# Full attention: values weighed for eight query blocks at once, with inverses kept in DRAM

## The reference, cut to what matters

```python
qkv = x @ w_qkv.T
qkv = qkv.reshape(b, t, dh, 3, h).transpose(3, 0, 4, 1, 2)     # t = 1024, h = 16 heads, dh = 64
q, k, v = (qkv[0], qkv[1], qkv[2])
scores = jnp.einsum('bhid,bhjd->bhij', q, k) * scale
rel = jnp.arange(t)[None, :] - jnp.arange(t)[:, None] + (t - 1)
bias = rel_bias[rel]                      # 255 rows; larger indices take the last row
scores = scores + bias.transpose(2, 0, 1)[None]
attn = jax.nn.softmax(scores, axis=-1)
out = jnp.einsum('bhij,bhjd->bhid', attn, v)
out = out.transpose(0, 2, 1, 3).reshape(b, t, h * dh)
return out @ w_out.T                      # x = x + ga * this
```

## Time and profile before

| what | value |
|---|---|
| median of three runs | 2606.95 us |
| lowest and highest | 2600.77 and 2609.22 us |
| the profiled execution | 2595.65 us |
| its span | 2593.9 us |
| busy over the whole span | PE 94%, DVE 83%, ACT 78%, POOL 59% |
| mean granted TensorE clock | 0.986 |

### The profile page before, as it was taken

One profiled execution on the slowest core, in us unless ns is written; L12 is line 12 of the kernel. 1 busy time (PEld: TensorE's weight loads), 2 busy tenths in 40 slices (PEclk: granted clock), 3 DMA queues, 4 the chain that ended last, 5 costly groups with the idle time before them and its releaser, 6 DMA issues. The chain is left out here.

```text
span 2593.9 us, 118567 instructions
## 1 busy us (share of the span) xinstructions
PE 2449.6 (94%) x52349; PEld 1966.9 (76%) x52349; DVE 2153.8 (83%) x2455; ACT 2034.3 (78%) x4077; POOL 1519.8 (59%) x1029
## 2 busy tenths in 40 slices
PE   6799999999999999999999999699999999997999
PEld 2478888888888888888888887467776776775787
DVE  5888888888888888888888886489898888885898
ACT  4788898889889899988888996667676666664776
POOL 3788887888888888888888884122222222222110
PEclk9999999999999999999999999899999999999999
DMA  3244433443444344334443332123232322221221
GB/s 96 51 99 94 109 78 93 94 108 84 98 94 111 82 94 99 95 84 94 101 97 83 91 85 60 43 48 68 46 70 50 67 47 66 51 57 31 83 74 41
DMA packets 275793, 202.01 MB, mean 78 GB/s; under 512 B 117568, under 2 KB 215880, under 8 KB 274248
## 3 DMA queue, kind: packets, MB, share of 16 engines
q1 hardware_dynamic: 275280, 194.42, 31.3%
HBM read 36.96 MB, written 1.11 MB: 15 GB/s over the span
## 5 line engine op out<-in xcount | busy, mean ns | idle before, releaser
L514 POOL TENSOR_TENSOR lt_t_sin<-lt_qk,lt_tab 128x512 f32<-128x512 f32 x384 | 685.1, 1805 | 225.1 <-DVE lt_qk L1296 222.8
L519 POOL TENSOR_TENSOR lt_qr<-lt_qr,lt_t_sin 128x1024 f32<-128x1024 f32 x192 | 457.7, 2384 | 28.1 <-POOL lt_t_sin L514 0.9
L2078 DVE TENSOR_REDUCE fa_neg_max<-bank 128x1 f32<-128x1024 f32 x256 | 301.6, 1220 | 90.7 <-PE bank L1875 89.1
L2000 ACT ACTIVATE fa_prob<-bank,fa_neg_max 128x1024 f32<-128x1024 f32 x128 | 142.6, 1114 | 215.7 <-DVE fa_neg_max L2078 163.4
L1901 PE MATMUL bank<-fa_prob_t,fa_v 32*64 32x128 f32 x16384 | 293.4, 276 | 16.8 <-issue 12.2
L1901 PEld LDWEIGHTS bank<-fa_prob_t,fa_v 32*64 32x64 f32 x16384 | 244.4, 130 | 78.1 <-issue 57.9
L2088 DVE STREAM_TRANSPOSE fa_prob_t<-fa_prob 128x1024 f32<-128x1024 f32 x256 | 302.1, 1218 | 0.0
L607 PE MATMUL bank<-lt_w_high,lt_x_high 128*128 128x512 f32 x576 | 262.2, 455 | 0.8 <-ACT lt_v_tok L1009 0.4
L977 ACT COPY lt_qk<-bank 128x512 f32<-128x512 f32 x384 | 224.5, 589 | 23.8 <-POOL lt_t_sin L514 2.8
L1296 DVE TENSOR_TENSOR lt_qk<-lt_qk,lt_rn 128x2048 f32<-128x2048 f32 x96 | 238.2, 2481 | 2.5 <-ACT lt_rn L1003 2.5
L1289 DVE TENSOR_REDUCE lt_ssq<-lt_qr 128x32 f32<-128x2048 f32 x96 | 218.9, 2281 | 24.7 <-ACT lt_qr L985 24.7
(11 more groups left out here) (260 smaller groups left out, 5857.0 us busy)
## 6 DMA issues: line engine op xcount, KB each, us to landing
lt_v<-lt_v_tok SPq DMA_DIRECT2D x576, 128.0 KB
fa_v<-fa_v_tok SPq DMA_DIRECT2D x256, 128.0 KB
lt_v<-lt_v_tok SPq DMA_DIRECT2D x192, 64.0 KB
lt_k_t<-lt_k_t SPq DMA_DIRECT2D x84, 128.0 KB, 2.9
lt_v<-lt_v SPq DMA_DIRECT2D x168, 64.0 KB, 2.1
lt_w_raw<-in_lt_wqkv_dram SPq DMA_DIRECT2D x36, 256.0 KB
ex_cw_all<-cw_kept SPq DMA_DIRECT2D x8, 1024.0 KB, 4.6
lt_x_s<-h_in SPq DMA_DIRECT2D x96, 64.0 KB, 2.8
```

What stands on the lines that cost most here:

```text
L514: pool.tensor_tensor(dst[:, :, i, :], src[:, :, 1 - i, :], tab[:, g // 2 % 2, 1, at:at + 32].unsqueeze(1).to_broadcast([P, HEADS, 32]), AL ...
L519: pool.tensor_tensor(qr[:, g % 2, half], qr[:, g % 2, half], t_sin[:, :], ALU.add).then_inc(S.rotated, 1)
L2078: dve.tensor_reduce(neg_max[:, u % 2, par:par + 1], bank[:, 2 * par:2 * par + 2, :].rearrange("p a n -> p (a n)"), AX.X, ALU.max, negate=T ...
```

## The change

`weigh_v` now takes a whole half at a time, one half later: half h = u // 8 - 1 is weighed in step u, four blocks of 32 keys in each step, with 256 moving columns (eight units of 32 queries). Accumulation is cut into three parts that end with the steps t = 2, 5 and 7 (`LASTS`); after each ACT copies 128x1024 out of banks 4 to 7 (into `h_mid`, a tile that is free in this layer), and POOL adds the copies (`add_att`). Weighing is not cut in pieces any more, and side jobs always follow it.

`prob_t` holds one half, with turned probabilities laid out by unit in even halves and by group of keys in odd ones, so that the units of the next half can take the places that weighing has just freed; `turn(u)` waits for the weighing of step u. The inverses of a half are turned in one 128x32 transposition and go to DRAM and back, broadcast to 64 partitions for each head, issued by SP behind `place_v`; widening, spreading by PE and their emptying on ACT go away. Jobs and outputs are at other steps and banks, and the stage has 146 steps instead of 136. The core of the diff:

```diff
-    UPQ = 4
-    QUADS = UNITS // UPQ
-    QPH = QB // UPQ
+    LASTS = (2, 5, 7)
+    OUTS = N // 256
     KB = N // 32
+    KBS = KB // QB
...
-        prob_t = buf("prob_t", [P, 2, 2, UPQ, N])
-        att = buf("att", [P, 4, P])
-        att_t = buf("att_t", [P, 2, CH])
+        prob_t = buf("prob_t", [P, 2, QB, QB, P])
+        att_t = buf("att_t", [P, 2, N])
...
+            half, t = u // QB + 1, u % QB
+            if half >= HALVES or t in (1, 5):
                 return []
-            first = JPH * half + 6 * (q % QPH) + max(0, 2 * (s - 1))
+            first = JPH * half + 2 * (0, 0, 1, 2, 3, 0, 4, 5)[t]
             return [first, first + 1]
 
         def outs_at(u):
-            q = u // UPQ - 2
-            return [2 * q, 2 * q + 1] if u % UPQ == 1 and 0 <= q < QUADS else []
+            half = u // QB - (3 if u % QB == 1 else 2)
+            first = OUTS * half + (2 if u % QB == 1 else 0)
+            return [first, first + 1] if u % QB in (1, 5) and 0 <= half < HALVES else []
...
+        def att_done(u):
+
+            return 3 * (u // QB - 1) + LASTS.index(u % QB) + 1
+
+        def att(part):
+            return h_mid[:, part, PAD:PAD + N].rearrange("p (a n) -> p a n", a=4)
...
+            if weighed_at(u) is not None and u % QB in LASTS:
+                eng.wait_ge(S.att, att_done(u))
...
+        STEPS = range(UNITS + 2 * QB + 2)
...
+                def widen_inverse(half):
+                    sp.wait_ge(S.inv_t, half + 1)
+                    if half >= 1:
+                        sp.wait_ge(S.inv_in, 32 * half)
+                    for a in range(4):
+                        sp.dma_start(inv_kept[:, 32 * a:32 * a + 32], inv_t[32 * a:32 * a + 2 * QB, :]).then_inc(S.inv_kept, 16)
+                    sp.wait_ge(S.inv_kept, 64 * (half + 1))
+                    if half >= 1:
+                        sp.wait_ge(S.att_t, half)
+                    for par in range(2):
+                        kept = inv_kept[QB * par:QB * par + QB, :].rearrange("(o u) q -> o (u q)", o=1)
+                        sp.dma_start(inv_all[HD * par:HD * par + HD, :], kept.to_broadcast([HD, N])).then_inc(S.inv_in, 16)
...
+                def add_att(half, n):
+                    pool.wait_ge(S.att, 3 * half + n + 1)
+                    if n == 2:
+                        pool.wait_ge(S.att_sum, 2 * half + 1)
+                    pool.tensor_tensor(att(0), att(0), att(1), ALU.add).then_inc(S.att_sum, 1)
+
+                def divide(half):
+                    pool.wait_ge(S.att_sum, 2 * half + 2)
+                    pool.wait_ge(S.inv_in, 32 * (half + 1))
+                    if half >= 2:
+                        pool.wait_ge(S.out, OUTS * (half - 1))
+                    pool.tensor_tensor(att_t[:, half % 2, :].rearrange("p (u a r) -> p a u r", u=QB, a=4),
+                                       att(0).rearrange("p a (u r) -> p a u r", u=QB),
+                                       inv_all[:, :].rearrange("p (u a r) -> p a u r", u=QB, a=4),
                                        ALU.mult).then_inc(S.att_t, 1)
...
+                def weigh_v(half, t):
+
+                    if t == 0:
+                        pe.wait_ge(S.turned, 2 * QB * (half + 1))
+                        pe.wait_ge(S.v, 256 * (half + 1))
+                    for i in range(KBS):
+                        kb, cols = KBS * t + i, slice(32 * i, 32 * i + 32)
                         for a in range(4):
                             rows = slice(32 * a, 32 * a + 32)
                             for par in range(2):
                                 d = slice(HD * par, HD * par + HD)
-                                mm = pe.matmul(bank[d, 4 + a, 0:P].rearrange("p (u r) -> p u r", u=UPQ),
-                                               v[rows, half % 2, kb, d],
-                                               prob_t[rows, q % 2, par, :, 32 * kb:32 * kb + 32],
-                                               start=kb == 0, stop=kb == KB - 1, skip_group_check=True)
-                    if n == 1:
-                        mm.then_inc(S.av, 1)
-
-                def spread_inverse(q):
-                    pe.wait_ge(S.wide_t, q + 1)
-                    if q == 0:
-                        pe.wait_ge(S.mean, 1)
-                    for a in range(4):
-                        rows = slice(32 * a, 32 * a + 32)
-                        for par in range(2):
-                            d = slice(HD * par, HD * par + HD)
-                            mm = pe.matmul(bank[d, 4 + a, P:2 * P].rearrange("p (u r) -> p u r", u=UPQ), mean_32[rows, :],
-                                           inv_t[rows, par, :, :], start=False, stop=True, skip_group_check=True)
-                    mm.then_inc(S.inv_all, 1)
+                                p = prob_t[rows, par, t, :, cols] if half % 2 else prob_t[rows, par, :, t, cols]
+                                mm = pe.matmul(bank[d, 4 + a, 0:JW].rearrange("p (u r) -> p u r", u=QB),
+                                               v[rows, half % 2, kb, d], p, start=i == 0 and t - 1 in (-1,) + LASTS,
+                                               stop=i == KBS - 1 and t in LASTS, skip_group_check=True)
+                    mm.then_inc(S.av, 1)
...
+                    half = weighed_at(u)
+
+
+                    fresh = u % QB in LASTS or half is None
                     if u + 1 < UNITS:
                         scores(u + 1)
                     wait_emptied(pe, u - 1)
-                    if s == 0:
-                        for j in jobs_at(u):
-                            job(j, fresh)
...
+                def empty_att(half, part):
+                    if half >= 1 and part < 2:
+                        act.wait_ge(S.att_t, half)
+                    if part == 2:
+                        act.wait_ge(S.att_sum, 2 * half + 1)
+                    act.copy(att(min(part, 1)), bank[:, 4:8, 0:JW]).then_inc(S.att, 1)
...
+                    half, j = u // QB, u % QB
+                    if half >= 1:
+                        dve.wait_ge(S.av, QB * (half - 1) + j + 1)
                     for par in range(2):
                         dve.wait_ge(S.probs, 3 * u + 1 + 2 * par)
-                        dve.transpose(prob_t[:, q % 2, par, u % UPQ, :], prob[:, u % 2, par, :]).then_inc(S.turned, 1)
-
-                def invert(q):
-
-                    r = row_sum[:, q % 2, :, :]
-                    dve.wait_ge(S.probs, 3 * UPQ * (q + 1))
+                        if half % 2:
+                            dve.transpose(prob_t[:, par, :, j, :], prob[:, u % 2, par, :].rearrange("p (g n) -> p g n", g=QB))\
+                               .then_inc(S.turned, 1)
...
+                def turn_inverse(half):
+                    dve.wait_ge(S.inv, half + 1)
+                    if half == 0:
+                        dve.wait_ge(S.cleared, 1)
+                    else:
+                        dve.wait_ge(S.inv_kept, 64 * half)
+                    dve.transpose(inv_t[:, :], inv_sum[:, :]).then_inc(S.inv_t, 1)
```

More of the change, by code:

```diff
@@ L1818, in add @@
                     pool.tensor_tensor(x, x, y[:, n % 2, :], ALU.add).then_inc(S.x, 1)
-                pool.memset(mean_32[:, :], 1.0 / 32).then_inc(S.mean, 1)
                 for i in LOWS:
@@ L1823, in _ @@
                 for u in STEPS:
-                    if u % UPQ == 1:
-                        if weighed_at(u) is not None:
-                            widen(weighed_at(u))
-                        for n in outs_at(u):
-                            add(n)
-                    if u % UPQ == 3 and weighed_at(u) is not None:
-                        divide(weighed_at(u))
+                    for n in outs_at(u):
+                        add(n)
                     for j in jobs_at(u):
@@ L1886, in scores @@
                     mm.then_inc(S.scores, 1)
-                def weigh_v(q, s, n):
-                    half = q // QPH
-                    lo, step = KB // UPQ * s, KB // UPQ // 2
-                    if s == 0 and n == 0:
-                        pe.wait_ge(S.turned, 2 * UPQ * (q + 1))
-                        if q % QPH == 0:
-                            pe.wait_ge(S.v, 256 * (half + 1))
-                    for kb in range(lo + step * n, lo + step * (n + 1)):
+                def weigh_v(half, t):
[4 more added lines that the diff above has]
+                        kb, cols = KBS * t + i, slice(32 * i, 32 * i + 32)
                         for a in range(4):
@@ L1926, in project_out @@
+                    mm.then_inc(S.av, 1)
+                def project_out(n, start):
+                    half = n // OUTS
+                    pair = half // B
+                    pe.wait_ge(S.att_t, half + 1)
+                    if n % (OUTS * B) == 0:
+                        pe.wait_ge(s_wo[pair % 2], 16 * (pair // 2 + 1))
+                    pe.matmul(out_bank(n), w_out[:, pair % 2, :], att_t[:, half % 2, n % OUTS * JW:n % OUTS * JW + JW],
```

(22 more changed lines are left out.)

135 lines of the change are left out of this document (40 added, 95 removed).

## The result

| what | before | after |
|---|---|---|
| median of six runs, same chip | 2601.18 us | 2629.34 us |
| lowest and highest | 2599.34 and 2609.22 | 2622.06 and 2637.63 |
| ratio, 95% interval | | 1.0099 [1.008, 1.0118] |
| the profiled execution, its span | 2595.65, 2593.9 us | 2625.08, 2623.3 us |

A forecast was written before the change was run, and what follows sets the result against it. Plain steps were taken as bound by the loop maxima, exponentials, scores, maxima (4.94 us). Steps -5.0, pauses -6.8 and tail +12.5 gave +0.7, or 2607.7 on the median, stated as 2606 us, range 2590 to 2626.

The forecast's parts named there:

- k1: Period between DVE's maxima in each half, holding sums and reciprocals: 5.39 us predicted, 5.00 before.
- k2: The next period of a half, PE's because weighing was cut around other matmuls: from 5.12 to 4.94 us.
- steps otherwise: Undisturbed half of eight periods: 42.20 us against 42.53, -0.33 each, -5.0 over 15 halves.
- tail: Stage end, where nothing covers weighing: eight steps instead of four, 33.1 us against 21.3, with 0.7 of pauses +12.5.
- rival E: Weighing cost is per record, 0.92 us a step instead of 1.76; faster, chance together with rival B 0.33.
- k7: Last period of a half, PE's because weighing was cut around other matmuls: from 5.36 to 4.94 us.
- rival B: Pauses vanish as PE uses code at half the rate, and emptying waits hide: -13.8, 2593 us, chance 0.29.
- Rival C: Pauses are not the code's, so none goes: +7.5, 2614 us, chance 0.14.
- Head: Stage start, where weighing begins four steps later and PE's longer rest may keep the clock low: 0, between -1 and +1.
- D: Odd halves' transposes, written as eight pieces, take 2.1 instead of 1.2 us: about +90, 2697 us, chance 0.06.
- F: The transposes' new wait for weighing decides in all steps, plain ones 5.17 us: +32, 2638 us, chance 0.10.
- A: The terms hold as summed: 2606 us, no change, chance 0.37.

The follow-up runs named there:

- one input: The changed kernel with DVE's two-input addition of row sums made a one-input reduction at the same place: 2595.60 us, ratio to before 0.9973.
- 128 columns: The changed kernel with each 256-column weighing matmul written as two of 128 columns: 2656.43 us, ratio to before 1.0199.
- head work: The changed kernel with inverses made in step 4, not 0, of a half, plus four unused PE matmuls in each of steps 1 to 7: 2586.00 us, ratio 0.9943.

## Why the prediction was wrong

**The step that failed** is that of k1: "so DVE has 2.49+2.27+0.46 and a transposition ... 5.39", together with "POOL ... Not on the path, except at the end". The 0.46 for sums and reciprocals was read in before, where POOL had nothing of length to do at that moment. The change puts a division of 2.36 us there, started by the last part sum, and DVE's addition of two SBUF operands stands until it ends: 1.75 instead of 0.13. k1 measured 7.05. With the hold taken away and nothing else, k1 is 5.43 (one input), and the sum of a half 42.00 against the 42.20 predicted. That this is the cause is shown by three repairs that touch different sides of it, and by the same hold planted in the kernel before. The Trainium skill has the rule (SBUF — State Buffer, SBUF: two separate sides): VectorE and GpSimd share a pair of ports that is locked for the whole instruction, taken by a VectorE operation with two SBUF inputs too, when the GpSimd operation reads SBUF, as the division does. The trace agrees to 0.03 us. It spoke against this change and was not weighed; the prediction asked of POOL only whether it was busy too much, not when.

**The account.** In us of the stage, relative to before; the sums of clean halves are those of one input:

| term | predicted | measured | worked out from |
|---|---|---|---|
| hold of the addition | 0 | +22.7 | 14 x (7.05 - 5.43) |
| slow scores in k2 | 0 | +8.6 | 7 halves, 42.8 instead of 7 x 4.88 |
| steps otherwise | -5.0 | -7.4 | 14 x (42.00 - 42.53) |
| disturbances, pauses for issue above all | -6.8 | -14.9 | 610.36 - 14 x 42.53 |
| first two halves | 0 | +3.0 | 49.22 - 47.06, 42.86 - 42.00 |
| tail | +12.5 | +16.4 | 44.9 - 28.5 |
| sum | +0.7 | +28.4 | stage: +28.6 |

**Slow scores** were in no step and no rival: PE's rest of 2.15, itself made by the hold, is followed in half of the cases by scores at the lower clock (granted 0.50). Without the rest they are gone from all halves (one input).

**Steps otherwise:** right within 0.2 of a half. Weighing of 64 records takes 1.98 in the profile where the old run of 128 took 2.10, as taken (the stream, not the record: rival E fell). The waits for the copies are 0.5 and cost what was said in k1 (with one input 5.43 for 5.39). Splits and spreading gave their time back (k2 4.88, k7 5.00).

**Pauses:** the direction was right, the size was not. "If pauses go with the code, 0.45 of 15.0" took them as in proportion; all went. The 15.0 is also more than the pauses: PE's waits for issue between unit 8 and unit 120 are 11.4 in 14, and the other 3.6 are longer periods for which no single cause was traced. That all went is rival B's first half. Rival C falls: the pauses went with half of the weighing's instructions and came back with them at 128 columns. That it is the fetching of the code that PE waits for fits, but is not shown. Nor are pauses in proportion to the code: 1.31 MB had none at all and 2.23 MB had 13.2 us. The Trainium skill's rule is that crossing a block of code is mostly hidden (Runtime: NRT & Kernel Launch, Instruction fetch mechanics). The changed kernel's trace agrees in full. Those of before and of 128 columns agree for most blocks, with 14 waits of PE for 132 pieces of all engines' code between unit 8 and unit 120 in the one, and 11 for 127 in the other, and these few are worth 11 to 14 us.

**Inverses through DRAM** cost nothing, as predicted; the broadcast lands in 4.0 us and no engine waits for it, not even when it starts four steps later.

**Head:** "I take 0, between -1 and +1" was +2.2, outside. The direction of the risk was named (a longer rest may keep the lower clock), and head work shows that the clock matters there. The size is that of one execution: the same work took 48.3 to 52.1 in the others.

**Tail:** 37.9 from the first weighing instead of 33.8. The order of the waits was right; weighing after PE's rests ran at the lower clock twice, (5.19 - 3.7) + (5.40 - 3.7) = 3.2 of the 4.1.

**The rivals.** D fell (1219 and 1220 ns). F gave a time near the measured one, 2638, by another way: the transposes waited for weighing only in k1, 0.19 each time, and plain steps stayed at 4.94. So the price was near by luck and the place wrong. No rival had an engine held by another that isn't on the path. With the hold alone taken away (one input) the ratio is 0.9973, 7 us faster than before: between A and B, and inside the range.

## What to carry to other kernels

When a change gives GpSimd long operations on SBUF, look at which VectorE instructions will run beside them, not at how busy GpSimd is; a tiny one with two SBUF inputs can cost the rest of the long one (1.62 us here, fourteen times), and a form with one input, a later place or shorter GpSimd instructions take that away. What a delay costs depends on whether the other engines have slack or arrears: two holds of 1.0 us cost 0.6 us a half in the kernel before, and one of 1.6 cost 1.6 and a slower clock in the change. Where TensorE is left with rests of 2 us between bursts, price the burst behind it at the lower clock as the other end of the range.

## What the runs showed of the hardware

- A VectorE addition of 128x8 with two SBUF inputs takes 0.13 us alone and 1.75 beside a GpSimd division that has 1.72 to go; a reduction with one input (0.13), and a reciprocal (0.25), beside it are not lengthened. Between two GpSimd instructions of one queue VectorE gets in (0.60 beside a subtraction of 0.71, with a second one behind it).
- Rests of TensorE of 2.13 to 2.15 us in an otherwise dense stretch were followed by matmuls at 0.79 and 0.63 instead of 0.50 and 0.40 in 7 of 14 cases, with the granted clock at 0.50. What decides between the cases was not found; the length of the rest does not, as the longest, 3.21 before 1770.01, was followed by scores at full clock.
- Work whose result is not used made the stage shorter, with the granted clock of the first half at 0.96 instead of 0.82: 44.86 us against 48.3 to 52.1.
- A blockwise transposition of 128x1024 that writes eight strided pieces takes as long as one that writes a row of 1024: 1219 and 1220 ns.
- Halving the number of matmul instructions at the same streamed columns took away all of TensorE's pauses for issue in the middle of the stage, 11.4 us in 14, and doubling it again brought 13.2 us in 9 back.
